# A mixture-of-experts kernel: one shared three-tile block ahead of each expert's program, and no DMA drain at block ends

## The reference

```python
x = x + tanh(g_xattn) * xattn(layernorm(x), ctx, ctx, ...)
# mixture of experts
xf = (layernorm(x) normalised again) * ln_gamma + ln_beta
top_v, top_i = top_k(clip(xf @ router_w.T), 2);  top_p = softmax over the two
# row r of expert e: the tokens that chose e, in order, the first C = 1280 kept
gu = einsum('ecd,efd->ecf', xb, w12);  g, u = split(gu, 2)
yb = einsum('ecf,edf->ecd', silu(g) * u, w3)
x = x + tanh(g_ffn) * sum over a token's two experts of weight * yb
```

## Time and profile before

| what | value |
|---|---|
| median of 3 runs | 2775.05 us (2775.0 to 2783.22) |
| the profiled execution, as timed | 2775.47 us |
| its span in the profile | 2773.5 us |
| TensorE busy | 96% of the span |
| mean granted TensorE clock | 0.982 |

### The profile page before, as it was taken

One profiled execution on the slowest core, in us unless ns is written; L12 is line 12 of the kernel. 1 busy time (PEld: TensorE's weight loads), 2 busy tenths in 40 slices (PEclk: granted clock), 3 DMA queues, 4 the chain that ended last, 5 costly groups with the idle time before them and its releaser, 6 DMA issues.

```text
span 2773.5 us, 41250 instructions
## 1 busy us (share of the span) xinstructions
PE 2660.9 (96%) x14422; PEld 2396.2 (86%) x14423; DVE 1397.2 (50%) x2725; ACT 979.8 (35%) x2543; POOL 415.9 (15%) x393
## 2 busy tenths in 40 slices
PE   6999999849999999999999999999999999999987
PEld 5888888739999888888888888888888999989987
DVE  5777777624444444444344444454444444444555
ACT  4766676422222322233222332232222322233343
POOL 4455554410000100011000200010000200030030
PEclk9999999969999999999999999999999999999999
DMA  7522222132101410123101321131111411033142
GB/s 261 201 83 76 93 84 74 68 134 85 46 24 54 108 43 26 45 60 84 45 23 45 78 91 48 66 68 66 45 40 32 117 46 45 23 84 125 68 124 79
DMA packets 60035, 208.40 MB, mean 75 GB/s; under 512 B 9564, under 2 KB 9836, under 8 KB 51602
## 3 DMA queue, kind: packets, MB, share of 16 engines
q1 hardware_dynamic: 43282, 175.30, 17.6%
q0 software_dynamic: 16640, 31.69, 5.9%
HBM read 145.60 MB, written 67.70 MB: 77 GB/s over the span
## 4 chain that ended last, share of the span: by engine, by line
PE 75%; issue 2%; DVE 1%; ACT 1%; DMA 0%; DVEq 0%; ACTq 0%; POOL 0%; POOLq 0%
PE bank L1414 74%; PE bank L1420 1%; DVE yacc L1354 0%; DMA raw<-in_moe_w_dram 0%; DVE slotsT_lo L1321 0%; DVE w_lo L1308 0%; ACT slotsT_hi L1233 0%; DVE h L1374 0%; ACT yout L1260 0%; ACT w_hi L1229 0%; ACT h_hi L1274 0%; DVE w_lo L1315 0%; POOL out_dram L1209 0%; ACT w_hi L1224 0%; ACT silu L1268 0%
## 5 line engine op out<-in xcount | busy, mean ns | idle before, releaser
L1414 PE MATMUL bank<-slotsT_hi,w_hi 128*128 128x384 f32 (+2 forms) x2560 | 886.6, 346 | 20.0 <-issue 12.1
L1414 PE MATMUL bank<-slotsT_lo,w_hi 128*128 128x384 f32 (+2 forms) x2560 | 884.3, 345 | 2.0 <-issue 2.0
L1414 PE MATMUL bank<-slotsT_hi,w_lo 128*128 128x384 f32 (+2 forms) x2560 | 882.8, 345 | 0.0
L1374 DVE TENSOR_TENSOR h<-silu,bank 128x384 f32<-128x384 f32 (+2 forms) x320 | 183.7, 574 | 828.1 <-PE bank L1414 818.1
L1414 PEld LDWEIGHTS bank<-slotsT_hi,w_hi 128*128 128x128 f32 x2560 | 482.8, 189 | 50.9 <-issue 13.7
L1414 PEld LDWEIGHTS bank<-slotsT_lo,w_hi 128*128 128x128 f32 x2560 | 482.9, 189 | 24.9
L1414 PEld LDWEIGHTS bank<-slotsT_hi,w_lo 128*128 128x128 f32 x2560 | 482.7, 189 | 23.6 <-issue 2.2
L1274 ACT CAST h_hi<-h 128x384 fp32r<-128x384 f32 (+2 forms) x320 | 169.2, 529 | 740.8 <-DVE h L1374 740.8
L1268 ACT ACTIVATE silu<-bank 128x384 f32<-128x384 f32 (+2 forms) x320 | 162.2, 507 | 723.8 <-PE bank L1414 723.5
L1354 DVE TENSOR_TENSOR yacc<-bank,yacc 128x512 f32<-128x512 f32 x464 | 316.8, 689 | 168.9 <-PE bank L1414 168.8
L1414 PE MATMUL bank<-w_hi,h_hi 128*128 128x512 f32 x1008 | 399.9, 397 | 0.3 <-DVE yacc L1354 0.3
(11 more groups left out here) (158 smaller groups left out, 2890.1 us busy)
## 6 DMA issues: line engine op xcount, KB each, us to landing
raw<-in_moe_w_dram SPq DMA_DIRECT2D x65, 1536.0 KB, 6.2
xrow<-expert_rows SPq DMA_DIRECT2D x42, 520.0 KB, 9.4
expert_rows<-zeros SPq DMA_DIRECT2D x40, 520.0 KB, 8.1
xin<-in_x_dram SPq DMA_DIRECT2D x16, 512.0 KB, 3.7
xres<-in_x_dram SPq DMA_DIRECT2D x16, 512.0 KB, 3.7
out_dram<-xres SPq DMA_DIRECT2D x16, 512.0 KB
probs<-in_L_xattn_Wq_dram SPq DMA_DIRECT2D x1, 1024.0 KB, 9.3
probs<-in_L_xattn_Wo_dram SPq DMA_DIRECT2D x1, 1024.0 KB, 6.4
```

The source lines that it names most:

```text
L1374: nc.vector.tensor_tensor(h32[q % 2][:, 0:W], silu[q % 2][:, 0:W], UB[q % 2][:, 0:W], ALU.mult)\
L1414: last = nc.tensor.matmul(out_ap, st, mv, start=(at == 0), stop=(at == n - 1))
```

## The change

Five edits stand together:

1. Both blocks are made with `no_gpsimd_drain=True`: GpSimd's drain of its DMAs at each block's end is left out.
2. Every tile count's first block has three tiles: 10 is (3, 3, 4) where it was (4, 3, 3), 7 is (3, 4) where it was (4, 3), 4 is (3, 1) for (2, 2), 8 is (3, 3, 2) for (4, 4). The other counts keep their blocks.
3. That first block of an expert's first chunk is written once, at the top of the loop (`shared=True`), ahead of the reading of the count; the comparisons and the branch stand behind it. The rest of the first chunk is in the programs.
4. In the shared block tiles 4 to 7 are transposed and split whatever the count, and units 0 and 1 of the next chunk's weights are split; `units_at` and `late_units` are changed in the first chunk to suit.
5. ScalarE computes one column of `silu` at the start of the second block, so that the function table is loaded there; the tables' loads in the programs are gone. The waits of `g1` on `silu_ready` and `h32_ready` at a chunk's start ask for one step less.

```diff
-            with nc.Block() as block:
+            with nc.Block(no_gpsimd_drain=True) as block:
...
-            BLOCKS = {3: (3,), 4: (2, 2), 5: (3, 2), 6: (3, 3), 7: (4, 3), 8: (4, 4), 9: (3, 3, 3), 10: (4, 3, 3)}
+            BLOCKS = {3: (3,), 4: (3, 1), 5: (3, 2), 6: (3, 3), 7: (3, 4), 8: (3, 3, 2), 9: (3, 3, 3), 10: (3, 3, 4)}
...
-            def units_at(nt, q):
+            def units_at(nt, q, first):
 
                 plan = {1: ((0, 1), (2, 3)), 2: ((0,), (1, 2), (3, 4), (5,)), 3: ((0,), (1,), (2,), (3,), (4,), (5,))}
+                if first and len(BLOCKS[nt]) < 3:
+                    plan = {1: ((0,), (1,)), 2: ((0,), (1,), (2, 3), (4, 5))}
                 return plan[len(BLOCKS[nt])][q]
 
-            def late_units(nt):
-                return (4, 5) if len(BLOCKS[nt]) == 1 else ()
+            def late_units(nt, first):
+                return ((2, 3, 4, 5) if first else (4, 5)) if len(BLOCKS[nt]) == 1 else ()
 
             def slots_at(nt, q, half):
 
                 at = {(0, 0): 0, (0, 1): 2, (2, 0): 4}.get((q, half))
-                return [] if at is None else [XA + i for i in (at, at + 1) if XA + i < nt]
+                return [] if at is None else [XA + i for i in (at, at + 1) if q == 0 or XA + i < nt]
+
+            def blocks_of(nt, first, shared):
+
+                return list(enumerate(BLOCKS[nt]))[slice(0, 1) if shared else slice(1 if first else 0, None)]
...
                     e = nc.snap(index, min_val=0, max_val=E - 1)
+                    chunk(TILES[0], e, 0, 0, 0, True, False, shared=True)
                     n_e = eng.value_load(counts[0:1, bass.ds(e, 1)], min_val=0, max_val=T)
...
                     act.sem_inc(yout_ready, NT)
+                    nc.scalar.activation(silu[0][:, 0:1], ident[:, 0:1], ACT.Silu)
                     act.wait_ge(raw_loaded[0], 16)
...
                                 elif not first:
-                                    pe.wait_ge(silu_ready, base)
+                                    pe.wait_ge(silu_ready, base - short(nt) - 1 + q)
```

More of the change, by code:

```diff
@@ L981, in flamingo_gated_layer @@
             XB = NT - XA
-            assert all(w[0] <= XA for w in BLOCKS.values())
+            XS = 4
+            assert all(w[0] == TILES[0] <= XA for w in BLOCKS.values())
             XL = 2 * P
@@ L1021, in flamingo_gated_layer, with short, step_of @@
             units_before = lambda e, c: e * (NCH * NU) + c * NU
-            def step_of(nt, q):
-                n = NJ * len(BLOCKS[nt])
-                return 1 + (STEPS - n if q == n - 1 else 0)
+            def short(nt):
+                return STEPS - NJ * len(BLOCKS[nt])
+            def step_of(nt, q, first, last):
+                n = 1 if first or q else 1 + short(nt)
+                return n + short(nt) if last and q == NJ * len(BLOCKS[nt]) - 1 else n
             def tile_of(nt, t):
@@ L1242, in _, with chunk @@
                         x_high(i, xa_tp, i + 1, xa_hi)
-                    def chunk(nt, e, c, par, half, first, last):
+                    def chunk(nt, e, c, par, half, first, last, shared=False):
                         base, tiles = steps_before(e, c), tiles_before(e, c)
@@ L1261, in scaled @@
                                                  scale=wslot[:, t:t + 1]).then_inc(yout_ready, tile_of(nt, t))
-                        for b, width in enumerate(BLOCKS[nt]):
+                        for b, width in blocks_of(nt, first, shared):
                             W = width * P
@@ L1268, in chunk @@
                                 nc.scalar.activation(silu[q % 2][:, 0:W], GB[q % 2][:, 0:W], ACT.Silu)\
-                                  .then_inc(silu_ready, step_of(nt, q))
+                                  .then_inc(silu_ready, step_of(nt, q, first, last))
                                 if first:
@@ L1278, in chunk @@
                                         x_high(i, xb_tp, XB * e + i - XA + 1, xb_hi)
-                                units(units_at(nt, q))
+                                units(units_at(nt, q, first))
                             if last and b == 0:
@@ L1285, in chunk @@
                                     scaled(t)
+                        if shared:
+                            return
                         if not last:
-                            units(late_units(nt))
+                            units(late_units(nt, first))
                         if first and nt < NT:
-                            act.sem_inc(xb_tp, min(XB, NT - nt))
+                            act.sem_inc(xb_tp, min(XB - XS, NT - nt))
                         if last:
@@ L1478, in g2 @@
                         def g2(t, b, earlier, y=None):
-                            of, at, hs, ws = (1 - par, tiles_before(e, c - 1), base, units) if earlier else \
+                            of, at, hs, ws = (1 - par, tiles_before(e, c - 1), base - short(nt), units) if earlier else \
                                 (par, tiles, base + NJ * b + NJ, units + NU)
@@ L1493, in g2 @@
                                 .then_inc(y_ready, down_of(nt, t))
-                        for b in range(nb):
+                        for b, _ in blocks_of(nt, first, shared):
                             g1(b)
+                            if shared:
+                                return
                             if last and b == nb - 1:
```

24 lines of the change are left out of this document (13 added, 11 removed).

## The result

The change took the median from 2777.62 us (20 runs, 2772.67 to 2783.22) to 2774.0 us (20 runs, 2770.74 to 2777.35), a ratio of 0.9986 with a 95% interval of 0.998 to 0.9993. The gain of 0.14% is clear of zero and under the 0.3% that the forecast took as a difference to be told. It is also inside the forecast's range, 2764 to 2781 us. The profiled execution took 2775.19 us, its span 2773.4.

A forecast was written before the change was run, and what follows sets the result against it. TensorE, busy 2660.9 of 2773.5 us, was taken as the bound, beside its idle places and block ends. Terms -9.45 - 1.4 + 1.05 + 2.9 + 0.4 + 2.7 + 3.0 = -0.8 us gave 2774 us, range 2764 to 2781.

The forecast's parts named there:

- Drains: GpSimd's drains at both block ends lie uncovered: -5.30 and -4.15, sum -9.45 us; low bound -5.30 only.
- The path behind the shared block: From count reading to first matmul, as long as before, only moved: 2.8 to 3.6 us TensorE idle behind the shared block.
- Expert 5: Its short branch becomes a 5 us fetch, 3.6 us idle for 0.69: +2.9; if code is still at hand, -0.7.
- Expert 3: Branch idle of 3.4 us for 2.79, plus one extra tile turn of 0.43: +1.05 us; closing costed separately.
- the rival's price: Idle time behind the shared block cools TensorE's clock: 1.9 us a fall, up to 2783 us in all; chance 0.09.
- Expert 7: Second chunk waits for weight units 2 and 3, now split behind ScalarE's and VectorE's branch: +2.7 us (+2.2 to +3.4).
- Closings: Experts 1 to 4 close with seven down products behind a four-wide block: 0.85 x 4 - 0.47, put at +3.0 us.
- The rival of gaps for ten-tile experts: Code behind the comparisons is late for ten-tile experts too: three more gaps of 3.5 us, 2784.7 us; chance 0.06.
- The late branch: Rival: code arrives while the shared block runs, so branches at experts 0, 3, 5, 6, 7 are cheap: 2755 us; chance 0.08.
- The last drain: Rival: the second block's drain time stays outside the span: +4.15, 2778 us; chance 0.08.
- the small terms: Rival: the closing costs nothing and expert 5 keeps its code: -7.4 in all, 2767.6 us; chance 0.12.
- Its own signs: Wrong if shared-block branches are short, a 0.50 clock shows behind them, or the first block's barrier isn't 5 us sooner.

The follow-up runs named there:

- code order: The changed kernel with the programs behind the ten-tile one laid out as 7, 9, 5, 3, 8, 6, 4 instead of 9 down to 3: 0.9969, 2767.59 us.
- combined ones with the shared block: Changed kernel with units 0 to 3 split in the shared block, two-block units respread, programs reordered: 2760.23 us; also with 10 tiles as (3, 4, 3): 2761.30 us.
- Drains only: The kernel before with both GpSimd block-end drains left out and nothing else: ratio 0.9975, 2769.98 us.
- First drain only: The kernel before with only the first block's GpSimd drain left out, the last one kept: ratio 0.9983, 2773.63 us.
- narrow ends: The changed kernel with 7 tiles as (3, 2, 2) and 10 tiles as (3, 4, 3): ratio 0.9994, 2774.43 us.
- widths only: The kernel before with 7 tiles as (3, 4) and 10 tiles as (3, 3, 4), no shared block, drains kept: ratio 1.0036, 2788.06 us.

## Why the prediction came out as it did

- **Drains.** Right: both rows gone, the barrier 5.3 us nearer to the last work, the tail 4.2 shorter. By medians the two together gave 7.7 of 9.45 us.
- **The path behind the shared block.** Right in kind, too dear. The step "it is as long as before, only moved" failed: the fetch ran beside few DMAs and took 3.4 to 3.6 us at experts 0, 6 and 7 where the sum had about 5. Hence expert 0 -2.9 for -1.4, and expert 6 -0.65 for +0.4, where the second wait for code of 2.04 us did not come back, as the sum had it.
- **Expert 5.** Wrong. "By its nearest rows, the four others, it is a 5 us fetch" should have gone by where the target lies: the branch stayed at 0.35 us, the 0.69 us idle of before went, -1.1 for +2.9. The low bound, -0.7, was the case. The order of the programs decides this (shown), though why the code stays at hand is open. The Trainium skill, "Runtime: NRT & Kernel Launch", section "Instruction fetch mechanics", has a taken branch outside a small window fetch its target first. The runs agree for targets far off. The forecast took from it that expert 5 loses its cheap branch, and that did not come: the nine-tile program stayed at hand over the shared block's 8 us of other code. How large the window is, no run here shows.
- **Expert 3.** Wrong by 4.5 us, by two terms. One was missing: the change of the widths was costed at the closing alone, though it puts four down products where three were from chunk to chunk; seven waits, about 0.5 us each by the distance of the matmuls' starts. The other was a rival: behind the idle time of 2.98 us the granted clock fell once, for 1.8 us; the rival's price was 1.9. Its reasoning, that the length of the idle time decides, did not hold: the clock fell behind 1.89 us in one trace of the same code and stayed at 1.00 behind 2.79 in the other. That it fell in this trace and not in that of before is in part luck.
- **Expert 7.** Right in mechanism: the second chunk waited for w_lo because units 2 and 3 moved behind the branch (shown). Sized at +2.7, it was +1.2; VectorE's fetch kept it idle for 2.94 us, where the sum went by ScalarE's 5.1 with its reading.
- **Closings.** Right: +0.75 and +0.7 at experts 2 and 4, forecast 0.85 each.
- **Expert 1.** Missing: the slow branch to the loop's top behind the nine-tile program delayed the first matmul (1.08 us idle). Of the 2.1 us, 1.35 went when that branch was short (code order, shown); the rest is the closing. The rival of gaps for ten-tile experts is not this: no comparison of theirs was slow.
- **The rivals.** The late branch was cheap at one expert of five. The last drain did not reappear. Of the small terms one fell away, expert 5's, and the closing's stayed.
- **Its own signs.** Of the three that were to show it wrong, the barrier came as forecast; a short branch and a clock of 0.55 were there, at one expert each.
- **Sums.** 0.85 x 4 - 0.47 is 2.9, not 3.0, and expert 6's 4.8 less 4.31 is 0.5, not 0.4; neither changes the forecast.

The misses outside expert 3 and 1 add up to -8.3 us, those two to +5.8: the total came out near by luck, because they offset each other. What was right for its reason is the drains' 9.5 us, the closing, and the kind of each wait behind the shared block but expert 5's.

What stays open: why the branch back to the top is slow behind one program and fast behind another (4.96 and 4.52 us behind nine tiles in the kernel after, 4.1 to 4.9 behind nine in the four other runs with the shared block and the old order of programs, 2.85 behind seven in the reordered one, 2.67 there in the combined ones with the shared block, at most 0.47 else; without the shared block never over 0.38). It moved with the code's place, but no run separated place, length and the hint ahead of the branch. Nor is it known what decides whether the clock falls behind an idle time of 1.8 to 3.1 us.

## What to carry to other kernels

A program that branches by size should be costed by where its targets lie: a branch to a program right behind the one run last cost 0.3 to 0.5 us here and one to any other program 3.3 to 6.3, so the order in which bodies are written is a free knob, worth 7.2 us here by the experts' times, where moving the branch was worth at most 2. When a block's width moves to another place, recount each engine's order in the steady chunks, not only at the edges: one 0.69 us piece ahead of an add cost about half a us at each of seven chunks. A block end that drains GpSimd behind DMAs already waited for gives its row's time back almost whole.

## What was not expected of the hardware

- The fetch behind the comparison that branches to an expert's program, where that lies far off: 3.3 to 3.8 us with a DMA share up to 0.16, 4.1 to 4.9 at 0.35 to 0.55, 3.9 to 5.1 at about 1.0, 6.0 to 6.3 at expert 0 with 381 GB/s and more.
- Code right behind the program that ran last stays at hand while a block of 48 matmuls and 16 transposes from elsewhere in the code runs (0.33 to 0.42 us).
- A branch back to a loop's top took 0.23 us behind one program and up to 4.96 behind another.
- The length of an idle time did not decide the clock here. Behind expert 3's branch it fell to 0.50 to 0.63 after 1.89 us (Drains only), 2.31 (First drain only), 2.83, 2.98, 3.19 and 3.44 us, and stayed at 1.00 after 2.53 (narrow ends), 2.79 (before) and 3.07 us (widths only). A fall cost about 1.7 us.
